# Second layer: a later place for the second attention's preparation, seven pieces of choosing, a copied reciprocal

## What is computed

```python
q = (x @ Wq) ; k = (x @ Wk)                    # 8 heads of 64
gl_v = (x @ Ws).reshape(b, t, h, 5)
wv = topk_mask(gl_v, 2) * sigmoid(gl_v)        # two of five experts, for each token and head
xv = einsum('btd,edk->btek', x, Wv)
v = einsum('bthe,btek->bhtk', wv, xv)
attn = softmax(q * scale @ k.T) @ v
mask_o = topk_mask(x @ Wd, 2)
out = einsum('bthe,bthk,ekd->btd', mask_o, attn, Wo)
```

## Time and profile before

| | us |
|---|---|
| median of three runs | 3017.31 |
| lowest, highest | 3007.75, 3017.68 |
| the profiled execution | 3025.34 |
| its span, first to last instruction | 3023.6 |
| TensorE busy in the span | 2443.8 |
| VectorE busy | 1941.5 |
| GpSimd busy | 1886.4 |
| ScalarE busy | 1686.8 |

### The profile page before, as it was taken

The page is one execution under the profiler, slowest core; times in us unless marked ns, Lnnn a source line. Parts: engine busy times, 40 slices in busy tenths (PEclk is TensorE's granted clock), DMA queues, the critical chain, the costliest instruction groups (busy, mean ns, idle before and its releaser), DMA issues. The chain is left out here.

```text
span 3023.6 us, 31386 instructions
## 1 busy us (share of the span) xinstructions
PE 2443.8 (81%) x10153; PEld 1137.3 (38%) x10153; DVE 1941.5 (64%) x3045; ACT 1686.8 (56%) x2384; POOL 1886.4 (62%) x1886
## 2 busy tenths in 40 slices
PE   4677777787877777645986999999999999999895
PEld 2222323332332332222553444444444444444443
DVE  3888979798979887521333665656565565746554
ACT  1688888888887889701222545444444444444350
POOL 0556577778767878745773036756556573846585
PEclk7677777778777877756997999999999999999996
DMA  3000000000000001015996000000000000000000
GB/s 98 15 1 8 10 15 16 15 17 15 16 15 17 15 10 22 9 23 162 281 263 145 1 1 1 1 15 7 15 8 15 8 1 21 1 8 1 8 1 14
DMA packets 95156, 99.12 MB, mean 33 GB/s; under 512 B 19824, under 2 KB 91760, under 8 KB 94960
## 3 DMA queue, kind: packets, MB, share of 16 engines
q1 hardware_dynamic: 70784, 74.12, 8.6%
q0 software_dynamic: 24176, 22.70, 4.1%
HBM read 74.30 MB, written 26.80 MB: 33 GB/s over the span
## 5 line engine op out<-in xcount | busy, mean ns | idle before, releaser
L850 POOL TENSOR_TENSOR TT<-TT,SS 128x512 f32<-128x512 f32 x512 | 649.4, 1303 | 204.4 <-ACT SS L780 203.9
L1541 ACT ACTIVATE PR<-S,NM 128x512 f32<-128x512 f32 x512 | 347.0, 683 | 577.7 <-DVE NM L1708 577.7
L1708 DVE TENSOR_REDUCE NM<-S 128x2 f32<-128x1024 f32 x256 | 312.8, 1222 | 287.0 <-PE S L1445 286.9
L370 PE MATMUL OB<-TT,VAL 128*17 128x512 f32 x1024 | 347.5, 788 | 53.2 <-ACT TT L788 53.1
L613 DVE TENSOR_SCALAR TT<-SC 128x1024 f32<-128x1024 f32 x256 | 311.3, 1216 | 76.8 <-PE SC L349 49.4
L855 POOL DMA_INDIRECT slot_tokens<-TID,IDX x256 | 256.1, 1000 | 143.1 <-issue 85.5
L615 DVE SCALAR_TENSOR_TENSOR SS<-SC,TT 128x1024 f32<-128x1024 f32 x256 | 313.6, 1225 | 20.6 <-issue 1.8
L1445 PE MATMUL S<-KT,QT 64*128 64x512 f32 x1024 | 307.1, 667 | 0.7 <-ACT QT L1510 0.7
L1474 PE MATMUL OT<-PT,VN 128*64 128x512 f32 x1024 | 285.1, 637 | 2.9 <-ACT PT L1547 2.1
L1456 PEld LDWEIGHTS TP<-ident,PR 128*128 128x128 f32 x2048 | 228.0, 142 | 147.7 <-issue 119.9
L1456 PE MATMUL TP<-ident,PR 128*128 128x128 f32 x2048 | 275.9, 278 | 6.2 <-DVE PT L1713 4.9
(11 more groups left out here) (258 smaller groups left out, 4143.2 us busy)
## 6 DMA issues: line engine op xcount, KB each, us to landing
WG<-w_gu SPq DMA_DIRECT2D x64, 384.0 KB
WD<-w_dn SPq DMA_DIRECT2D x64, 128.0 KB
stream<-rows SPq DMA_DIRECT2D x1, 4224.0 KB, 16.8
XL<-x SPq DMA_DIRECT2D x8, 512.0 KB
X<-x SPq DMA_DIRECT2D x8, 512.0 KB
rows<-XL SPq DMA_DIRECT2D x8, 512.0 KB
slot_tokens<-TID,IDX POOLq DMA_INDIRECT x256
stream<-X SPq DMA_DIRECT2D x8, 512.0 KB
```

Source lines behind the costliest of these rows:

```text
L370: ins = pe.matmul(OB[r:r + DH0 + 1, :], values_of[:, mt, h, :], TT[:, h % RING, mt, :], start=(mt == 0), stop=(mt == NT - 1))
L850: ins = pool.tensor_tensor(tt[:, mt, :], tt[:, mt, :], ss[:, mt, :], ALU.add)
L1541: act.activation(PR[s % 2][h2][:], S[s % 2][:, h2, :], ACT.Exp, bias=NM[:, s % 2, h2:h2 + 1], accum_out=SM[:, pair % 2, j, h2:h2 + 1]).the ...
L1708: dve.tensor_reduce(NM[:, s % 2, :], S[s % 2][:], AX, ALU.max, negate=True).then_inc(sems["peak"], 1)
```

## The change

Five tables or functions change.

- `PREP_2`: turn_norm, gates, experts, queries2 and keys2 stand a step later (a few change the slot), choose has numbers 0 to 6 in steps 6 to 11 in place of 0 to 3 in steps 6 to 9, and mix_values stands in step 11 in place of 9.
- `OUT_1`: product_out1 number 0 goes from slot 1 to slot 2 of step 0. `OUT_2`: product_out2 goes from (2,1), (2,2), (3,2), (4,1) as step and slot to (2,2), (3,1), (3,2), (4,2).
- `PREP_2_LATE`: only choose has new places.
- `choose` is cut into seven: two with two comparisons each, four with one addition and one subtraction each (the last of them with the 1 added to the exponentials), and one with the masks and WV.
- `shares` in a kind 1 run: the reciprocal writes eight values to RS, and after a drain a copy broadcasts them to RB.

```diff
-OUT_1 = table((0, 0, 1, "product_out1", 0), (0, 1, 1, "product_out1", 1), (0, 1, 2, "product_out1", 2),
+OUT_1 = table((0, 0, 2, "product_out1", 0), (0, 1, 1, "product_out1", 1), (0, 1, 2, "product_out1", 2),
               (0, 2, 1, "product_out1", 3), (0, 2, 3, "stats", 1))
 PREP_2 = table(
-    (0, 4, 1, "turn_norm", 0), (0, 5, 1, "turn_norm", 1), (0, 5, 2, "gates", 0),
-    (0, 6, 1, "experts", 0), (0, 6, 2, "experts", 1), (0, 6, 3, "sigmoid", 0), (0, 6, 3, "choose", 0),
-    (0, 7, 2, "experts", 2), (0, 7, 3, "choose", 1), (0, 8, 1, "experts", 3), (0, 8, 3, "choose", 2),
-    (0, 9, 1, "queries2", 0), (0, 9, 2, "keys2", 0), (0, 9, 3, "choose", 3),
-    (0, 9, 3, "mix_values", 0), (0, 9, 3, "mix_values", 1), (0, 9, 3, "mix_values", 2), (0, 9, 3, "mix_values", 3),
-    (0, 10, 1, "queries2", 1), (0, 10, 2, "keys2", 1), (0, 11, 2, "queries2", 2), (0, 12, 1, "keys2", 2),
-    (0, 13, 1, "queries2", 3), (0, 13, 2, "keys2", 3))
+    (0, 5, 1, "turn_norm", 0), (0, 6, 1, "turn_norm", 1), (0, 6, 2, "gates", 0), (0, 6, 3, "choose", 0),
+    (0, 7, 2, "experts", 0), (0, 7, 3, "sigmoid", 0), (0, 7, 3, "choose", 1), (0, 8, 1, "experts", 1),
+    (0, 8, 2, "experts", 2), (0, 8, 3, "choose", 2), (0, 9, 1, "experts", 3), (0, 9, 3, "choose", 3),
+    (0, 10, 1, "queries2", 0), (0, 10, 2, "keys2", 0), (0, 10, 3, "choose", 4),
+    (0, 11, 1, "queries2", 1), (0, 11, 2, "keys2", 1), (0, 11, 3, "choose", 5), (0, 11, 3, "choose", 6),
+    (0, 11, 3, "mix_values", 0), (0, 11, 3, "mix_values", 1), (0, 11, 3, "mix_values", 2), (0, 11, 3, "mix_values", 3),
+    (0, 12, 2, "queries2", 2), (0, 13, 1, "keys2", 2), (0, 14, 1, "queries2", 3), (0, 14, 2, "keys2", 3))
...
-    (0, 10, 1, "experts", 0), (0, 10, 2, "experts", 1), (0, 10, 3, "sigmoid", 0), (0, 10, 3, "choose", 0),
-    (0, 11, 2, "experts", 2), (0, 11, 3, "choose", 1), (0, 12, 1, "experts", 3), (0, 12, 3, "choose", 2),
-    (0, 13, 1, "queries2", 0), (0, 13, 2, "keys2", 0), (0, 13, 3, "choose", 3),
+    (0, 10, 1, "experts", 0), (0, 10, 2, "experts", 1), (0, 10, 3, "sigmoid", 0), (0, 9, 3, "choose", 0), (0, 10, 3, "choose", 1), (0, 10, 3, "choose", 2),
+    (0, 11, 2, "experts", 2), (0, 11, 3, "choose", 3), (0, 11, 3, "choose", 4), (0, 12, 1, "experts", 3), (0, 12, 3, "choose", 5),
+    (0, 13, 1, "queries2", 0), (0, 13, 2, "keys2", 0), (0, 13, 3, "choose", 6),
...
 OUT_2 = table((0, 0, 1, "turn_out2", 0), (0, 1, 1, "turn_out2", 1), (0, 1, 2, "turn_out2", 2),
-              (0, 2, 1, "product_out2", 0), (0, 2, 2, "product_out2", 1), (0, 3, 2, "product_out2", 2),
-              (0, 4, 1, "product_out2", 3))
+              (0, 2, 2, "product_out2", 0), (0, 3, 1, "product_out2", 1), (0, 3, 2, "product_out2", 2),
+              (0, 4, 2, "product_out2", 3))
...
-                    for s in range(1, SE):
+                if i in (0, 1):
+                    for s in (2 * i + 1, 2 * i + 2):
                         dve.tensor_tensor(CM[:, s - 1, :, 0:SE - s], GL[:, :, 0:SE - s], GL[:, :, s:SE], ALU.is_ge)
                     dve.drain()
-                if i in (1, 2):
-                    for s in (2 * i - 1, 2 * i):
-                        dve.tensor_tensor(CN[:, :, s:SE], CN[:, :, s:SE], CM[:, s - 1, :, 0:SE - s], ALU.add)
-                        dve.drain()
-                        dve.tensor_tensor(CN[:, :, 0:SE - s], CN[:, :, 0:SE - s], CM[:, s - 1, :, 0:SE - s], ALU.subtract)
-                        dve.drain()
-                if i == 2:
+                if 2 <= i < 2 + SE - 1:
+                    s = i - 1
+                    dve.tensor_tensor(CN[:, :, s:SE], CN[:, :, s:SE], CM[:, s - 1, :, 0:SE - s], ALU.add)
+                    dve.drain()
+                    dve.tensor_tensor(CN[:, :, 0:SE - s], CN[:, :, 0:SE - s], CM[:, s - 1, :, 0:SE - s], ALU.subtract)
+                    dve.drain()
+                if i == SE:
...
-                if i == 3:
+                if i == SE + 1:
...
-                    dve.reciprocal(RB[:], SM[:, pair % 2].rearrange("p j h -> p (j h)").unsqueeze(2)
-                                   .to_broadcast([P, 2 * NT, DH1])).then_inc(sems["rs"], 1)
+                    dve.reciprocal(RS[:, pair % 2], SM[:, pair % 2])
+                    dve.drain()
+                    dve.tensor_copy(RB[:], RS[:, pair % 2].rearrange("p j h -> p (j h)").unsqueeze(2)
+                                    .to_broadcast([P, 2 * NT, DH1])).then_inc(sems["rs"], 1)
```

## The result

The changed kernel takes 2980.3 us (median of four runs, 2976.23 to 2985.86); the kernel before takes 3014.36 beside it (median of four). The ratio is 0.9877, with a 95% interval of 0.9852 to 0.9903. So it is faster by 1.2%, about half of what was forecast, and lies above the range.

The account below looks back on a forecast made before the run. TensorE sets the pace, its long holes paid twice through the clock. First-attention runs 45.0, second-attention 24.6, runs 0 and 1 4.0: 73.6 us off, from the median 3017.31 to 2944, range 2920 to 2972.

Parts of the forecast that it names:

- The hole before turn_norm: First-attention step 4, TensorE waiting for XN: 4.5 us cut to 0.8, plus 2.7 of clock, 6.4 us a run.
- the hole behind turn_out2: Second-attention runs, product_out2 waiting for AT: 2.66 us and 1.4 of clock saved, 4.1 a run; 0.5 returns at spread.
- The three hand-overs of BK: New TensorE waits at product_out1, queries2 and product_out2 directly behind heads2 or spread: 0.84, 0.8 and 0.5 us.
- Runs 0 and 1: Four places where turns waited for PT behind the reciprocal: 4.0 us saved in all.
- the two bounds: VectorE's broadcast copy inside SBUF: between 192 ns (eight-element instruction) and 684 ns (copy from PSUM).
- mix_values was never late: Answers a rival, chance 0.03: mixing too late for the second attention's first attend, about 3025 us; forecast had 22 us cover.
- I count no hole: Step 6, choose's two comparisons with turn_norm and the GL copy: no TensorE wait, as gates' 16 products run there.
- VectorE gives up 2.4 to 2.9 us each: The cheaper reciprocal of eight sums: VectorE time saved per reciprocal, 79 to 95 us in all, nearly all beside TensorE's work.
- rival 4: The copy fights GpSimd for SBUF, as dear as the old reciprocal: 66 us gain, 2952; chance inside the forecast's 0.80.
- sign of failure: Numerators wait longer for VectorE's peaks because choose is packed into steps 6 and 11; no size given.
- It comes behind scores, attend, heads2 and the next turns: turn_norm moved one step later in first-attention runs: 3.7 us more cover, leaving 0.8 of the 4.5 us wait.
- a net gain of 0.5: Step 0, product_out1 number 0 behind attend: 1.35 us wait for OS goes, 0.84 us bank hand-over comes.

Follow-up runs that it names:

- e1: The changed kernel with GpSimd's long addition GO = GO + GT cut into four of 320 columns: 2953.33 us, ratio 0.9795 to the kernel before.
- e5: A separate kernel without the computation, six VectorE instruction forms timed beside GpSimd partners: SBUF copy and two-input addition 0.426 us alone, mean 2.5 beside the long addition.
- e3: The changed kernel with both turn_norm parts back in steps 4 and 5: 2999.75 us, ratio 0.9951 to the kernel before.
- e6: The changed kernel with product_out1 number 0 back in slot 1 of step 0: 2972.44 us, ratio 0.9842 to the kernel before.
- e7: The changed kernel with GpSimd's addition in four except batch 6, product_out1 number 0 back, queries2, keys2 number 1 and product_out2 moved off spread: 2942.2 us, ratio 0.9738.
- e2: The changed kernel with the broadcast reciprocal of 3.34 us back in place of reciprocal, drain and copy: 2999.66 us, ratio 0.9935 to the kernel before.

## Why the prediction was wrong

*Right.* The hole before turn_norm closed in six runs, and the clock stays up in both kinds of run. The second-attention runs: the hole behind turn_out2 went and 0.5 us came back at spread. The three hand-overs of BK cost 0.84, 0.69 and 0.51 us for forecasts of 0.84, 0.8 and 0.5. Runs 0 and 1 gave 5.1 us (148.2 to 143.1, from the first turn) for 4.0. The copy itself, not held, takes 0.43 us, between the two bounds that were given (0.19 and 0.68). mix_values was never late: no wait for VN appears on TensorE.

*Wrong, first step: "I count no hole"* (choosing in seven pieces, step 6), and with it "VectorE gives up 2.4 to 2.9 us each" (2.2 were given up, as the copy has a mean of 0.92 us). The prediction had the row for it, the addition of 1.18 us beside its twin of 0.43, and used it for the copy alone, as rival 4. It never asked which instructions of choose would meet GpSimd's four additions of 2.9 us in their new places. In the changed kernel the comparisons' mean went from 641 to 1183 ns and the subtractions' from 386 to 845. In TensorE's waits this is 0.55 us for XT (behind the held copy), 1.29 for XV and 1.48 for PT (behind held choose) in run 5, 3.3 us; e1 removed 2.6 of it on average, and e5 shows the mechanism by itself. The prediction named this sign of failure itself, exponentials that wait for the maxima, but gave the packing of choose as its reason; packing is the smaller part, since e1 leaves 3.9 of the 9.1 us for XV and 1.3 of the 9.7 for PT. Rival 4's arithmetic (66 us of gain at worst) was wrong for the same reason: it priced the copy and not choose.

*Wrong, second step: what a moved part leaves behind.* "It comes behind scores, attend, heads2 and the next turns" counted the cover that turn_norm gains, and not the cover that attend loses. 0.8 us were to be left in step 4 and 1.53 were, for another engine; in step 0 a net gain of 0.5 was to come from product_out1 and a loss of 0.4 came (1.35 before, 0.89 + 0.84 after). Together 1.6 us a run, and 0.4 more in step 12 for the same reason. That slot 1 hides these waits is shown from both sides: a part put back there removes the 1.53 us (e3), the 0.89 (e6, e7) and the 0.4 (e7). What e6's move is worth in time is too small to measure.

*The sum.* Per pair 11.6 us were forecast and 6.8 measured, 4.8 less. The unforeseen 3.3, 1.6 and 0.4 us make 5.3 us of holes (7.7 for 2.4). Against them the clock gave back 4.6 us of TensorE's busy time in a pair (156.64 to 152.06), where 4.1 were counted. Six pairs lose 29 us of the 73.6. That leaves 45: in the two profiled executions the second layer is 45 us shorter, the first two stages are 3 us longer, and their totals differ by 42.2 (3025.34 and 2983.19). That the remainder fits so well is partly luck: runs 0 and 1 alone gave 1.1 us more than their term. The medians differ by 34.1. The profiled execution of before stood 11 us above its median and that of after 3 us, so the rest of the gap, some 8 us, is the spread of executions, which the prediction took as an offset that stays the same in both kernels.

*What stays open.* The medians of e1 and e3 don't fit their second layers (27 us for 12, and 19 for 31). In the profiled executions the first two stages explain it: with the same code they take from 1635.5 us (e3) to 1652.3 (the changed kernel), the shorter ones at a granted clock of 0.79, the longer ones at 0.77 to 0.78. Why the clock differs there from one execution to the next is open. Open is also what makes it fall or not behind the same idle times of 1.4 to 1.8 us (e2, e3).

## What to carry to other kernels

Before moving VectorE work, list what GpSimd runs in the new place: a two-input SBUF instruction or a fast copy inside SBUF that begins under a GpSimd instruction ends just behind it, so cut long GpSimd instructions, or let VectorE read one input from PSUM. When a part is moved out from between two dependent instructions, price the wait that it used to cover as well as the one that it escapes. In a kernel where TensorE is nearly always busy, count the clock with a hole: one of 4.5 us cost 2.7 more behind it. Closing it in six runs was worth 31 us of the second layer (e3), more than the copied reciprocal with its 71 us of VectorE time (20 us, e2). And compare the layer that an edit touches as well as the whole time: here stages that no edit touched differed by 17 us.

## What was unexpected of the hardware

A broadcast copy of eight fp32 values to 512 inside SBUF takes 0.426 us, as a dense one does, against 3.353 for the reciprocal in the same shape and 0.692 for a copy from PSUM. Beside a one-input GpSimd instruction of 3.45 us both copies have a mean of 3.27 us and the two-input addition one of 1.74, which is 0.43 and 3.06 in turn: the one-input form on GpSimd holds VectorE too. Of two instructions that collide the one that began first goes on, and VectorE's ends 0.28 us behind GpSimd's when it was the later one (0.17 us before its end in the case of 3.06). The reciprocal, with both sides in SBUF, is never held (3353 ns beside every partner).
